# A relu of Z folded into a maximum, and a centring moved from VectorE to ScalarE, in a fused GCN, LSTM and GNN kernel

## What is computed

```
h  = relu(LN(x))
h  = relu(adj @ (h @ Wg0 + bg0))          # U = h adj^T first, then Z = Wg0^T U
h  = relu(adj @ (h @ Wg1 + bg1))          # Y = h Wg1 + bg1, then V
for p in 1..4:                            # an LSTM over windows of p positions
    h[:, last position of each window] = last hidden state
x  = x + h
h  = relu(LN(x))                          # "second layer norm"
x  = x + diag(adj)·(h W[0]) + triu(adj) (h W[1]) + tril(adj) (h W[2]) + bias
```

## Time and profile before

| | us |
|---|---|
| median of 3 executions | 406.62 (406.6 to 406.8) |
| the profiled execution, its own time | 406.77 |
| span of that execution in the trace | 404.7 |
| TensorE matmul busy in the span | 395.7 (98%) |
| VectorE busy | 346.6 (86%) |
| ScalarE busy | 287.7 (71%) |
| GpSimd busy | 40.9 (10%) |

### The profile page before, as it was taken

The page is one execution under the profiler, slowest core; times in us unless marked ns, Lnnn a source line. Parts: engine busy times, 40 slices in busy tenths (PEclk is TensorE's granted clock), DMA queues, the critical chain, the costliest instruction groups (busy, mean ns, idle before and its releaser), DMA issues.

```text
span 404.7 us, 6549 instructions
## 1 busy us (share of the span) xinstructions
PE 395.7 (98%) x2386; PEld 343.7 (85%) x2386; DVE 346.6 (86%) x872; ACT 287.7 (71%) x579; POOL 40.9 (10%) x43
## 2 busy tenths in 40 slices
PE   7999999999999999999999999999999999999997
PEld 6787889898887889899777879899797788989774
DVE  5568999997989898887998898988898888788796
ACT  4767775685898676777589676777589677767553
POOL 4910003000200003000110000300120000000140
PEclk9999999999999999999999999999999999999999
DMA  7820000000000000000000000000000000000003
GB/s 236 316 100 2 1 0 2 1 2 2 0 1 2 27 28 0 28 0 2 3 0 26 28 0 28 0 28 2 0 1 28 0 28 26 2 27 2 1 2 130
DMA packets 5215, 11.18 MB, mean 28 GB/s; under 512 B 1088, under 2 KB 2112, under 8 KB 4672
## 3 DMA queue, kind: packets, MB, share of 16 engines
q1 hardware_dynamic: 5184, 10.77, 7.3%
HBM read 6.57 MB, written 4.19 MB: 27 GB/s over the span
## 4 chain that ended last, share of the span: by engine, by line
PE 80%; DVE 12%; ACT 5%; DMA 1%; issue 1%; POOL 0%; SPq 0%; ACTq 0%; DVEq 0%
PE PS L513 11%; PE PS L522 11%; PE PS L514 10%; PE PS L545 6%; PE PS L542 6%; PE PS L541 6%; PE PS L591 5%; PE PS L462 4%; PE PS L472 4%; PE PS L439 4%; PE PS L454 4%; PE PS L580 3%; PE PS L582 3%; PE PS L581 3%; ACT GT L846 2%; PE PS L555 2%
## 5 line engine op out<-in xcount | busy, mean ns | idle before, releaser
L846 ACT ACTIVATE GT<-PS,BG 128x256 f32<-128x256 f32 (+2 forms) x312 | 158.0, 564 | 16.4 <-PE PS L545 12.4
L513 PE MATMUL PS<-HH,WIH 128*128 128x256 f32 (+2 forms) x312 | 107.3, 345 | 1.8 <-DVE HH L997 1.8
L514 PE MATMUL PS<-HH,WIL 128*128 128x256 f32 (+2 forms) x312 | 102.7, 330 | 0.0
L522 PE MATMUL PS<-HL,WIH 128*128 128x256 f32 (+2 forms) x294 | 97.3, 331 | 0.6
L852 ACT ACTIVATE TC<-CS 128x512 f32<-128x512 f32 (+2 forms) x88 | 45.4, 515 | 49.5 <-DVE CS L973 36.2
L513 PEld LDWEIGHTS PS<-HH,WIH 128*128 128x128 f32 x312 | 58.8, 188 | 11.6 <-DVE HH L1004 4.3
L381 POOL TENSOR_TENSOR RS<-VE,NHALF 128x4 f32<-128x4 f32 (+2 forms) x17 | 29.2, 1720 | 352.3 <-DVE VE L918 273.9
L514 PEld LDWEIGHTS PS<-HH,WIL 128*128 128x128 f32 x312 | 58.9, 189 | 3.9 <-issue 1.2
L522 PEld LDWEIGHTS PS<-HL,WIH 128*128 128x128 f32 x294 | 55.5, 189 | 6.6 <-DVE HL L1012 2.4
L545 PE MATMUL PS<-SL,WHH 128*128 128x256 f32 (+2 forms) x192 | 60.1, 313 | 0.1
L541 PE MATMUL PS<-SH,WHH 128*128 128x256 f32 (+2 forms) x192 | 59.9, 312 | 0.0
(11 more groups left out here) (97 smaller groups left out, 651.8 us busy)
## 6 DMA issues: line engine op xcount, KB each, us to landing
out_tbd<-X SPq DMA_DIRECT2D x15, 256.0 KB, 2.0
X<-x_tbd SPq DMA_DIRECT2D x3, 1024.0 KB, 13.0
X<-x_tbd SPq DMA_DIRECT2D x4, 256.0 KB, 4.0
WI<-wih_t SPq DMA_DIRECT2D x1, 1024.0 KB, 5.2
WH<-whh_t SPq DMA_DIRECT2D x1, 768.0 KB, 6.8
out_tbd<-X SPq DMA_DIRECT2D x2, 128.0 KB, 1.7
WL<-w_l SPq DMA_DIRECT2D x1, 192.0 KB, 6.6
WG<-wg SPq DMA_DIRECT2D x2, 64.0 KB, 3.2
```

The source lines that it names most:

```text
L513: pe.matmul(dst, WIH[:, p - 1, cols], x_high, start=True, stop=False)
L514: pe.matmul(dst, WIL[:, p - 1, cols], x_high, start=False, stop=False)
L522: mm = pe.matmul(dst, WIH[:, p - 1, cols], x_low, start=False, stop=(j == 0))
L846: act.activation(GT[:, s, q, 0:n], bank(s, q)[:, 0:n], ACT.Tanh if q == C else ACT.Sigmoid, bias=BG[:, 4 * (p - 1) + q:4 * (p - 1) + q + 1 ...
```

## The change

1. Z is no longer summed with BG0T and then put through relu. VectorE writes max(Z, -BG0T) in one instruction (FLOOR0 = -BG0T is new), and ScalarE's relu_z is gone. Since relu(Z + b) = max(Z, -b) + b, the missing b is put through Wg1 once: YBIAS = BG0T^T Wg1 + bg1, and bias_y adds YBIAS in place of bg1. TensorE's Y waits for VectorE's maximum. At the start there is one new matmul (BG0T by Wg1, into bank (0, 2)) and there are two new VectorE instructions (FLOOR0, YBIAS), with waits between them.
2. VectorE's centring of quads 2 and 3 in groups 1 to 3's units (two instructions per group) is gone. ScalarE centres them batch by batch: batches 8 and 9 after unit 5's tanh, 10 and 11 after unit 6's, 12 and 13 after unit 8's, 14 and 15 after unit 9's. VectorE's add_bias, which overwrites the x that the centring reads, now waits for ScalarE for all four quads. The centring of the last group stays on VectorE.

```diff
-START_LATE = {4: ((OWN, 0),), 5: ((CENTRE, 2), (SHIFT, 0)), 6: ((SHIFT, 1), (SHIFT, 2))}
+START_LATE = {4: ((OWN, 0),), 5: ((SHIFT, 0),), 6: ((SHIFT, 1), (SHIFT, 2))}
...
-    quads=QUADS, between=START_BETWEEN, mid=START_MID, late={**START_LATE, 9: ((CENTRE, 3), (SHIFT, 3))})
+    quads=QUADS, between=START_BETWEEN, mid=START_MID, late={**START_LATE, 9: ((SHIFT, 3),)})
...
+CENTRE_UP_AT = {5: (8, 9), 6: (10, 11), 8: (12, 13), 9: (14, 15)}
...
                 for n in range(HB):
                     if n % PACK == 0:
-                        pe.wait_ge(h1_ready, 2 * HBANKS * g + s * HBANKS + n // PACK + 1)
+                        pe.wait_ge(z_sb, 2 * HBANKS * g + s * HBANKS + n // PACK + 1)
...
                 if g == GROUPS - 1:
-                    pe.wait_ge(centred, ON_SCALAR * g + q + 1)
-                elif q < ON_SCALAR:
-                    pe.wait_ge(turned_up, ON_SCALAR * g + q + 1)
+                    pe.wait_ge(centred, q + 1)
                 else:
-                    pe.wait_ge(centred, ON_SCALAR * g + q - ON_SCALAR + 1)
+                    pe.wait_ge(turned_up, QUADS * g + q + 1)
...
             pe.wait_ge(bias_ready, 2)
+            pe.matmul(bank(0, 2)[:, 0:D], BG0T[:, :], WG1[:, :], start=True, stop=True).then_inc(ybias_mm, 1)
+            pe.wait_ge(bias_ready, 3)
             graph_z(1, 0, False)
+            pe.wait_ge(bias_ready, 4)
             graph_y(0, 0)
...
-            def relu_z(s, g):
-
-                for n in range(HBANKS):
-                    act.wait_ge(z_sb, 2 * HBANKS * g + s * HBANKS + n + 1)
-                    part = Z[:, s, 512 * n:512 * n + 512]
-                    act.activation(part, part, ACT.Relu).then_inc(h1_ready, 1)
...
-            def centre_up(g, q):
-
-                if q == 0:
-                    act.wait_ge(var2, 2 * STREAMS * g + 1)
-                for b in range(q * PACK, (q + 1) * PACK):
+            def centre_up(g, batches):
+
+                for b in batches:
+                    if b % HB == 0:
+                        act.wait_ge(var2, 2 * STREAMS * g + 2 * (b // HB) + 1)
                     done = act.activation(H3[:, b, :], X[:, g * G + b, :], ACT.Relu, bias=MINUS2[:, b:b + 1])
-                done.then_inc(turned_up, 1)
+                    if b % PACK == PACK - 1:
+                        done.then_inc(turned_up, 1)
...
+                    if plan and k in CENTRE_UP_AT:
+                        centre_up(i - 1, CENTRE_UP_AT[k])
...
             def next_graph(i):
-                for part in (copy_u, relu_z):
-                    part(0, i + 1)
-                    part(1, i + 1)
-                for q in range(ON_SCALAR):
-                    centre_up(i, q)
+                copy_u(0, i + 1)
+                copy_u(1, i + 1)
+                centre_up(i, range(HB))
...
-                                      BG0T[:, :].unsqueeze(1).broadcast_to([128, PACK, T]),
-                                      ALU.add).then_inc(z_sb, 1)
+                                      FLOOR0[:, :].unsqueeze(1).broadcast_to([128, PACK, T]),
+                                      ALU.max).then_inc(z_sb, 1)
...
-                                      BG1[:, :].unsqueeze(1).broadcast_to([128, PACK, D]),
+                                      YBIAS[:, :].unsqueeze(1).broadcast_to([128, PACK, D]),
...
             def add_bias(g, q):
 
-                if q < ON_SCALAR and g < GROUPS - 1:
-                    dve.wait_ge(turned_up, ON_SCALAR * g + q + 1)
+                if g < GROUPS - 1:
+                    dve.wait_ge(turned_up, QUADS * g + q + 1)
...
-            dve.wait_ge(bias_ready, 2)
+            dve.tensor_scalar(FLOOR0[:, :], bank(1, 0)[:, 0:T], BG0[:, 0:1], -1.0,
+                              ALU.mult, ALU.mult).then_inc(bias_ready, 1)
+            dve.wait_ge(bias_ready, 3)
             bias_z(0, 0)
+            dve.wait_ge(ybias_mm, 1)
+            dve.tensor_tensor(YBIAS[:, :], bank(0, 2)[:, 0:D], BG1[:, :], ALU.add).then_inc(bias_ready, 1)
             bias_z(1, 0)
+            dve.wait_ge(bias_ready, 4)
             bias_y(0, 0)
```

More of the change, by code:

```diff
@@ L86 @@
 FILL = {4: 6, 9: 6, 15: 5}
-LOW, OWN, ADD, CENTRE, SHIFT = "low", "own", "add", "centre", "shift"
+LOW, OWN, ADD, SHIFT = "low", "own", "add", "shift"
 LAST = QUADS - 1
@@ L111 @@
     f_after={**START_F, 16: (VALUE, 12), 17: (VALUE, 13), 18: (VALUE, 14), 19: (VALUE, 15)},
-    quads=QUADS, between=START_BETWEEN, mid=START_MID, late={**START_LATE, 9: ((CENTRE, 3), (SHIFT, 3))})
+    quads=QUADS, between=START_BETWEEN, mid=START_MID, late={**START_LATE, 9: ((SHIFT, 3),)})
 LATE = Plan(at=START, f_after={**START_F, 16: (TURN, 3), 17: (SUM, 2)}, quads=LAST,
-            between=START_BETWEEN, mid=START_MID, late={**START_LATE, 9: ((CENTRE, 3), (SHIFT, 3))})
+            between=START_BETWEEN, mid=START_MID, late={**START_LATE, 9: ((SHIFT, 3),)})
 PLANS = (None,) + (GROUPS - 2) * (STEADY,) + (LATE,)
@@ L198, in program @@
         BG0T = sb("BG0T", [D, T])
+        FLOOR0 = sb("FLOOR0", [D, T])
+        YBIAS = sb("YBIAS", [T, D])
         BG1 = sb("BG1", [T, D])
@@ L235, in program @@
         rowsum_mm = sem("rowsum_mm")
+        ybias_mm = sem("ybias_mm")
         bn1 = sem("bn1")
@@ L248, in program @@
         z_sb = sem("z_sb")
-        h1_ready = sem("h1_ready")
         y_mm = sem("y_mm")
@@ L817, in _ @@
             copy_u(1, 0)
-            relu_z(0, 0)
-            relu_z(1, 0)
             high_h(0, 0)
@@ L1046, in centre @@
             def centre(g, q):
[L1048 to L1051, removed]
+                wait_apart(dve, var2, 2 * STREAMS * g + 2 * q + 2, x_quarter[0], 16)
                 part = bass.ds(g * G + q * PACK, PACK)
@@ L1126, in last_step @@
                     return
-                if what == CENTRE:
-                    centre(g, q)
-                elif what == SHIFT:
+                if what == SHIFT:
                     add_bias(g, q)
```

## The result

The changed kernel takes 408.14 us (median of 7, 407.56 to 408.26) against 406.62: a ratio of 1.0035, 95% interval 1.0025 to 1.0045. A second series of runs gave 407.74 against 406.50, 1.0028 (1.0017 to 1.0039). An interval that holds 1 leaves open whether there is a difference; these two do not hold it. The changed kernel is slower by about a third of a per cent. Its profiled execution took 408.26 us, that of before 406.77.

A forecast was written before the change was run, and what follows sets the result against it. The prediction took TensorE's nearly hole-free matmul queue as the bound, other engines counting only where TensorE waits for their results. Terms 0.13 - 0.63 + 0.76 + 1.08 = +1.34 us gave 408.0 us, range 406.1 to 409.0.

The forecast's parts named there:

- Start of group 0: Start: one added matmul, partly falling into an existing TensorE hole, FLOOR0 and YBIAS hidden; net +0.13 us.
- Boundary: Three group boundaries: Y's matmuls no longer wait for ScalarE's relus; gain 0.21 us each, 0.63 in all.
- the naive count of four relus: Boundary: counting four removed ScalarE relus as 2.5 us gain, which the prediction called wrong because ScalarE is idle before them.
- VectorE's side: Units 5 and 9: six centrings removed from VectorE bring 0, covered by waits; at most 0.6 us each otherwise.
- ScalarE after unit 5: Two centrings before value 5's copy delay TensorE by 0.40, 0.18, 0.18 us in groups 1 to 3; +0.76 us.
- ScalarE after unit 8: Two centrings delay value 8's copy and gate F of unit 10; 0.36 us a group, +1.08 for three groups.
- ScalarE after units 6 and 9: Centrings there cost nothing: after unit 6 idle time just fits them, after unit 9 value 9's copy waits for TensorE.
- Nothing takes the delays back: Units: the next waits, hidden state to TensorE, begin at TensorE's own last matmul of a unit and move with it.
- ScalarE has room: Rival: centring pairs disappear in ScalarE's slack, leaving only boundary and start; -0.5 us, 406.1; chance 0.19.
- VectorE was the limit: Rival: in units 5 and 9 gates and sums wait for VectorE's queue; relief gives 402.5 to 405; chance 0.08.
- The delays add up: Rival: value 5's and 8's copies cost 0.70 us per group, or unit 10's gates move; up to +3.7, 410.3; chance 0.10.
- YBIAS stalls the start: Rival: YBIAS and its waits at the start add up to 0.9 us more, 408.9; included in the range.

The follow-up runs named there:

- both_late: Changed kernel with batches 8 to 11 centred after unit 6's tanh and 12 to 15 after unit 9's; 406.19 us, ratio 0.9992 to the kernel before.
- unit5_late: Changed kernel with the centring of batches 8 and 9 moved from unit 5 to unit 6; 407.25 us, ratio 1.0017 to the kernel before.
- unit8_late: Changed kernel with the centring of batches 12 and 13 moved from unit 8 to unit 9; 406.96 us, ratio 1.0009 to the kernel before.
- pair_only_b: Kernel before plus two unread ScalarE centrings after unit 8's tanh in groups 1 to 3, VectorE's centring kept; 407.53 us, ratio 1.0026.
- centre_only: Kernel before with only the change's second half, centring moved to ScalarE, relu of Z left on ScalarE; 408.46 us, ratio 1.0046.
- double_centre: Kernel before with each VectorE centring in units 5 and 9 done twice; 406.45 us, ratio 0.9998.
- max_pad: Kernel before with only the change's first half, each of 16 dropped relus replaced by a one-column ScalarE activation; 406.19 us, ratio 0.9995.

## Why the prediction was right

Forecast 408.0 (406.1 to 409.0), measured 408.14 and 407.74.

- **Start of group 0.** Predicted +0.13, found +0.22 - 0.10 + 0.07 = +0.19. YBIAS and its waits are hidden: the matmul at 15.30, YBIAS at 15.72 (0.29 long, priced at 0.34), wanted at 17.24. The 0.07 before V was not in the forecast. V's first weight load, at 19.15, waits 0.15 us for VectorE's first sum of Y, which comes 0.54 us later than before (18.41 for 17.87) while TensorE's Y is only 0.46 late; why the sum loses the rest stays open.
- **Boundary.** Predicted -0.21, found -0.22, -0.24, -0.22; the naive count of four relus would have given ten times that.
- **VectorE's side, credited with 0.** Shown from both sides: with the work gone the idle times grew (1.24 to 2.00, 0.27 to 0.91) and both_late shows no gain at these places; doubling the work changed nothing either.
- **ScalarE after unit 5.** Predicted 0.40, 0.18, 0.18; found 0.37, 0.19, 0.19; unit5_late takes them away.
- **ScalarE after unit 8.** Predicted 0.36, found 0.33, 0.33, 0.34. The moved copy is 0.59 late, and value 9's own wait vanishes, as worked out. unit8_late takes the steps away, pair_only_b makes them alone. The sign named for it, a wait of some 0.6 us before gate F, is there: 0.45 on the matmul, 0.73 on its weight load.
- **ScalarE after units 6 and 9.** Predicted 0, found no step, even with four centrings there.
- **Nothing takes the delays back.** Held: but for drifts of a few hundredths each step stays to the end of the trace.
- **What I missed**: the start's 0.25 us between the two profiles. The steps at the places that the forecast prices add up to +1.26, beside a forecast of +1.34; the trace's +1.52 is that, the open part of the start (0.25, and 0.08 ahead of it), and the drifts. That the medians' +1.52 and +1.24 lie so close to +1.34 is in part luck, since they differ by 0.28 between themselves and the errors at the single places (0.01 to 0.06) partly cancel.

The rival "ScalarE has room" is refuted by centre_only, which loses 1.9 us, and "VectorE was the limit" by double_centre. "The delays add up" would have cost 0.70 us at each place; the steps are 0.17 to 0.37. "YBIAS stalls the start" asked for up to 0.9 us more; it is 0.19 in all.

## What to carry to other kernels

These runs show it for one kernel in which TensorE's queue is full: work taken from or given to the other engines has no price of its own; it has one at each place where the full engine waits for what stands behind that work in the queue. Read the engine's queue right behind the insertion: with an idle stretch of the inserted length before the next result that is wanted, it is free, and one place further along can decide between a loss and nothing. A delay often removes the next wait on the same engine, so take that off.

## What the runs showed of the hardware that I had not expected

Taking 16 instructions out of ScalarE's program made one of its copies, at 384 us, start 0.3 us late in each of three profiles, with an instruction load near it where before and max_pad have one some 20 us earlier; 16 dummy activations in their place removed the hole and gave 0.25 us back (406.19 against 406.44). An edit can so lose or gain a quarter of a microsecond where it changed nothing. The cause is open.

A TensorE wait of a few hundredths of a microsecond cost about 0.1 more here, since the matmul after it was also late. In the changed kernel value 6's first matmul is 0.07 us late at 226.42, and the next follows at 226.70, 0.28 us later, where these matmuls otherwise follow at 0.17; the step is 0.17 to 0.19. The third Z product shows the same: its second pass is late by 0.07 as well.
